# A transformer layer on one core: GpSimd adds the projection bias between its two normalisations, ScalarE copies the router logits ahead of the next hT

## What is computed

```python
q, k, v = jnp.moveaxis(qkv, 2, 0)
attn = jnp.einsum('bhnd,bhmd->bhnm', q, k) * SCALE
attn = attn * (1.0 - temperature[None] * eye)
attn = jax.nn.softmax(attn, axis=-1)
out = jnp.einsum('bhnm,bhmd->bhnd', attn, v)
out = out.transpose(0, 2, 1, 3).reshape(b, n, c)
return out @ w_proj + b_proj
...
h = _layernorm(h + _L0_attn_ref(h, ...), axis=-1)
...
scores = jnp.sqrt(jax.nn.softplus(flat @ gate_w))
_, indices = jax.lax.top_k(scores + gate_bias, K)
```

## Time and profile before

| | |
|---|---|
| runs | 801.5, 804.45, 809.3 us; median 804.45 |
| span of the profiled execution, first to last instruction | 762.7 us |
| PE (TensorE matmul) busy | 625.1 us, 82% |
| DVE (VectorE) busy | 480.6 us, 63% |
| ACT (ScalarE) busy | 321.7 us, 42% |
| POOL (GpSimd) busy | 189.1 us, 25% |
| mean granted TensorE clock | 0.896 |

### The profile page before, as it was taken

The page is one execution under the profiler, slowest core; times in us unless marked ns, Lnnn a source line. Parts: engine busy times, 40 slices in busy tenths (PEclk is TensorE's granted clock), DMA queues, the critical chain, the costliest instruction groups (busy, mean ns, idle before and its releaser), DMA issues.

```text
span 762.7 us, 15902 instructions
## 1 busy us (share of the span) xinstructions
PE 625.1 (82%) x4762; PEld 463.4 (61%) x4763; DVE 480.6 (63%) x1125; ACT 321.7 (42%) x564; POOL 189.1 (25%) x162
## 2 busy tenths in 40 slices
PE   4979788979797975488887999999999999999600
PEld 2665656756665665365655777777777777777500
DVE  0365756466757576557696566666666666677816
ACT  1433534444454545254533354444544445444200
POOL 1121524142424242423775000000000000006752
PEclk9989895989898987588999899999999999999855
DMA  6141422233333323242222011111111111112213
GB/s 250 52 161 38 140 90 89 76 119 90 119 90 119 90 72 105 79 131 60 82 83 71 23 42 43 36 36 36 41 43 36 36 36 40 44 37 71 79 52 97
DMA packets 51383, 57.85 MB, mean 76 GB/s; under 512 B 14544, under 2 KB 47728, under 8 KB 50080
## 3 DMA queue, kind: packets, MB, share of 16 engines
q1 hardware_dynamic: 47792, 50.22, 21.7%
q0 software_dynamic: 3568, 7.33, 3.3%
HBM read 41.78 MB, written 15.75 MB: 75 GB/s over the span
## 4 chain that ended last, share of the span: by engine, by line
PE 47%; issue 27%; POOL 14%; DVE 6%; ACT 2%; DMA 2%; POOLq 1%; SPq 0%; DVEq 0%; ACTq 0%
PE bank L632 20%; PE bank L651 9%; POOL dbuf L1434 5%; PE bank L642 5%; POOL stage L1450 4%; PE bank L500 4%; POOL arena L1376 3%; PE bank L485 2%; PE bank L540 2%; PE bank L558 2%; PE bank L620 1%; DMA con<-consts 1%; DVE arena L910 1%; POOL arena L1385 1%; DVE arena L948 1%
## 5 line engine op out<-in xcount | busy, mean ns | idle before, releaser
L632 PE MATMUL bank<-W,arena 128*128 (+1 forms) x1220 | 212.7, 331 | 0.0
L632 PEld LDWEIGHTS bank<-W,arena 128*128 128x128 f16 x1220 | 120.9, 99 | 74.7 <-issue 4.7
L651 PE MATMUL bank<-W,arena 128*128 (+1 forms) x1098 | 103.7, 250 | 8.9 <-DVE arena L1123 8.9
L1450 POOL DMA_INDIRECT stage<-ybuf,pos x36 | 36.1, 1002 | 287.6 <-DMA ybuf<-arena 277.0
L651 PEld LDWEIGHTS bank<-W,arena 128*128 128x128 f16 x1098 | 94.4, 100 | 17.9 <-DVE arena L1123 10.3
L1123 DVE SCALAR_TENSOR_TENSOR arena<-bank,sct,arena 128x384 f16<-128x384 f32 x86 | 49.1, 612 | 74.8 <-ACT arena L840 74.8
L485 PE MATMUL bank<-arena,par 128*96 128x288 f32 x192 | 69.0, 452 | 10.5 <-DMA con<-consts 10.1
L1137 DVE SCALAR_TENSOR_TENSOR arena<-arena 128x384 f32<-128x384 f32 x122 | 68.1, 558 | 4.2
L834 ACT ACTIVATE arena<-bank,sct 128x384 f32<-128x384 f32 x86 | 50.0, 581 | 43.1 <-PE bank L632 41.6
L642 PE MATMUL bank<-con,arena 128*128 128x128 f32 x366 | 54.5, 282 | 13.8 <-issue 8.2
L1132 DVE TENSOR_SCALAR arena<-bank,sct 128x384 f32<-128x384 f32 x86 | 58.2, 677 | 9.3 <-PE bank L632 9.1
(11 more groups left out here) (146 smaller groups left out, 883.4 us busy)
## 6 DMA issues: line engine op xcount, KB each, us to landing
stage<-w_all SPq DMA_DIRECT2D x9, 1344.0 KB, 6.0
arena<-xT SPq DMA_DIRECT2D x8, 864.0 KB, 4.9
stage<-w_all SPq DMA_DIRECT2D x9, 768.0 KB, 4.9
arena<-dbuf SPq DMA_DIRECT2D x43, 96.0 KB, 1.9
ybuf<-arena SPq DMA_DIRECT2D x43, 96.0 KB, 1.6
dbuf<-arena SPq DMA_DIRECT2D x6, 672.0 KB, 6.4
xbuf<-arena SPq DMA_DIRECT2D x8, 216.0 KB, 2.3
arena<-xbuf SPq DMA_DIRECT2D x18, 96.0 KB, 2.0
```

What stands on the lines that cost most here:

```text
L632: m = pe.matmul(bank[2 * k + n][:, 0:I // 2], xT16[:, b, lo, tail, :], W16[:, bass.ds(off + at + col, I // 2)], start=(z == 0), stop=(z == ...
L651: m = pe.matmul(bank[6][:, 0:C], hhT[:, lo, ic, :], W16[:, bass.ds(off + at + ic * C, C)], start=(ic == 0 and z == 0), stop=(ic == IC - 1 ...
L1450: PO.indirect_dma_start(fin[:, k % FS, c, :], None, ybuf[:, :], bass.IndirectOffsetOnAxis(ap=pos[:, c, k:k + 1], axis=0)).then_inc(s_f[k % ...
```

## The change

Two steps move; nothing is added or removed.

1. GpSimd's `h0b_out(g)` moves from the end of group g-1 (behind `weights_sum(g)`) into group g, between `normalise(g, 0)` and `normalise(g, 1)`. For group 0 it moves from the start of the program to the same place in group 0.
2. ScalarE's `logits_out(g-1)` moves ahead of `hT_out(g+1)`.

```diff
@@ ScalarE
                 weights_hi(g, (0,))
+                if not start:
+                    logits_out(g - 1)
                 if not last:
                     hT_out(g + 1)
-                if not start:
-                    logits_out(g - 1)
                 exps(g, 1)
@@ GpSimd
             def group(g, start=False, last=False):
                 normalise(g, 0)
+                h0b_out(g)
                 normalise(g, 1)
                 if not start:
                     scores_sqrt(g - 1)
...
                 if not last:
                     weights_sum(g + 1)
-                    h0b_out(g + 1)
-
-            h0b_out(0)
+
             weights_sum(0)
             group(0, start=True)
```

## The result

The changed kernel takes **823.85 us** (median of 4 runs, 816.66 to 828.54) against 806.88 us (4 runs, 801.5 to 809.7) of the kernel before: ratio **1.0203, interval 1.0136 to 1.0269**. The forecast was 812.0 with a range from 800.5 to 819. The profiled execution of the changed kernel took 819.69 us, its span is 817.9. Timed again later against the kernel before it took 779.88 us (773.08 to 790.13) against 767.53 (757.94 to 775.88), ratio 1.0177, interval 1.0097 to 1.0257. It is slower by about 2%, twice. Ratios and their intervals leave out runs more than 1.5% above the fastest of the same kernel; medians and ranges are of all runs.

What follows compares the result with a forecast made beforehand. It took the attention turn to be bound by GpSimd's chain, then VectorE, nearly tied with TensorE. Groups 1 to 6 net +9.3, group 0 +0.7, group 7 -2.5: +7.5 us on 804.45 gives 812.0 us, range 800.5 to 819.

Steps and rivals of the forecast that it cites:

- before's one long turn: Group 2 of the kernel before: clock stayed at 0.50, turn 44.00 us; its 6.0 us excess was subtracted from the sum.
- GpSimd's R stays: R is when GpSimd is free after the weights' sum, 7.08 us behind it; moving the bias was priced at nothing there.
- Transposes some 1.3 us behind R, second hole of 2.5 to 3: TensorE, groups 1 to 6: transposes start earlier, after the first normalisation, then wait 2.5 to 3 us before the projection.
- Projection at 4.05 in its first run, a fast turn of +1.4: TensorE, groups 1 to 6: first projection wholly at 1.2 GHz, 4.05 instead of 3.20 us; +1.4 us per group.
- too late for it: Clock returning 3.6 to 4.4 us after the first projection starts would not speed that projection, 4.05 us at 1.2 GHz.
- How often the clock stays down: Groups 1 to 6: one in four turns, 1.5 long episodes, each 4.6 us over a +1.4 turn.
- Group 0 at +0.7: Group 0: hT of group 1 newly waits for the bias, second exponentials come 0.5 to 1.0 us later; +0.7 us.
- Group 7 at -2.5: Last group: first normalisation no longer behind the bias, TensorE starts 2.4 to 4.2 us earlier; -2.5 us.
- Long episodes in most groups: Rival: clock fails to return in four of six groups' second runs; +19 us, 823.5 us, chance 0.1.
- The clock survives: Rival: TensorE's clock does not fall over two short holes, no turn is cold; -4.3 us, 800 us, chance 0.12.

Runs made afterwards that it cites:

- bias first: Kernel before, with GpSimd's bias ahead of the weights' sum instead of behind it: 762.21 against 767.53 us, ratio 0.9973.
- logits only: Kernel before, with only ScalarE's copy of the logits moved ahead of hT and GpSimd's order kept: 799.23 against 803.03 us, ratio 0.998.
- last group only: Kernel before, with the bias between the two normalisations in the last group alone: one run, 752.6 us against a median of 767.53.
- only GpSimd's half: Changed kernel with hT ahead of the logits again, so only the bias is moved: 820.72 against 803.03 us, no ratio.
- one hole instead of two: Changed kernel with one more wait: TensorE waits for hT ahead of the transposes, so they join the projection: 810.97 against 803.03 us, ratio 1.012.
- two holes filled: Changed kernel with useless identity transposes, 10 behind the router and 19 between transposes and projection: 809.92 against 803.03 us, ratio 1.0116.
- three holes filled: Changed kernel with identity transposes in TensorE's two holes and also ahead of the second half's transposes: 770.37 against 764.21 us, no ratio with an interval.
- sum on TensorE: Kernel before, with two matmuls with a matrix of ones replacing GpSimd's reduction for groups 0 to 7: 745.36 against 764.21 us, ratio 0.9769.
- filler in the kernel before: Kernel before with the logits ahead of hT and 34 identity transposes between router and transposes: 765.82 against 764.21 us, ratio 0.9989.
- router moved: Kernel before with the weights' sum on TensorE, logits ahead of hT, router matmuls ahead of the last score matmul: 749.03 against 767.53 us, ratio 0.981.
- the three kernels without its reduction: Weights' sum on TensorE: in the kernel before (0.9769), in the changed kernel (0.9708), in the kernel before with early logits and earlier router matmuls (0.981).

## Why the prediction was wrong, step by step

The sum of my terms was +7.5 us. To the root of group 7 the profiles give +18.4.

| term | forecast | profile | again |
|---|---|---|---|
| group 0 | +0.7 | +4.3 | +5.5 |
| fast turns of groups 1 to 6, 6 x (mean of the fast - 37.55) | +8.4 | +7.4 | +7.6 |
| long turns' excess over the fast | 1.5 x 4.6 = +6.9 | 3 x 4.96 = +14.9 | 2 x 4.82 = +9.6 |
| before's one long turn | -6.0 | -6.45 | -6.45 |
| group 7 | -2.5 | -1.75 | -2.6 |
| sum | +7.5 | +18.4 | +13.6 |

(37.55 is the mean of before's five fast turns. The fast turns of the changed kernel average 38.79 in the first profile, 38.81 in the second; 43.75 and 43.64 are its long ones. Group 0 again: 65.84 - 60.39; group 7 again: 35.78 - 38.37.)

- **GpSimd's R stays**: right. 14.49 against 14.47 us behind the root; the experiment with the bias first shows 6.70 us behind the sum with no bias there.
- **Transposes some 1.3 us behind R, second hole of 2.5 to 3**: the first right in four of six turns (1.28 to 1.29 us), 1.78 in group 3 (163.41 - 161.63, behind a normalisation of 1.64) and 1.68 in group 5. The second hole is 1.76 to 3.00. That the transposes are slow in every turn was wrong: in three of six they ran at 0.93 to 1.03.
- **Projection at 4.05 in its first run, a fast turn of +1.4**: right in size (+1.24), and four of the seven fast turns of both profiles (38.93 to 39.86) went as told, with the clock back in the second run. Wrong in "too late for it": in the other three (38.03 to 38.43) the clock comes back at the end of the first projection (group 4: L500 4.06, then L558 1.39), which I had ruled out.
- **How often the clock stays down**: this is the step that failed. "One in four, for six groups" gave 1.5 long turns; the profiles have 3 and 2 of six. I counted eight cold runs of before with two failures, but those runs were transposes and projection unbroken, behind one hole. The fraction belonged to a pattern that the change abolishes, and I carried it over without a row of the new one. Four profiles in the old order (before, logits only, bias first, last group only) have 2 long turns in 24; the two of the changed kernel 5 in 12. The cut of the run isn't the whole reason: joined again, with the bias still moved, the clock missed the first projection in five of six turns.
- **Group 0 at +0.7**: failed too. I priced the later exponentials and put the clock at nothing, though the earlier trace rows show a cold run there and hT was a new wait. The clock stayed down in it: +4.3 and +5.5. The root is at 64.68 to 67.73 us in the four profiles with the bias moved, the sum on GpSimd and no filler, and at 60.38 and 59.39 with filler. Of the 10.9 us that the first profile has beyond the forecast the long turns are 8.0, group 0 is 3.6, the fast turns are -1.0 and the rest is 0.3.
- **Group 7 at -2.5**: right sign, -1.75 and -2.6; the normalisation took 2.73 us beside L1065 in the first profile, so it is the late end of my bounds that came. The last-group-only kernel has -1.6.
- **The rivals.** "Long episodes in most groups" (four of six, 823.5, chance 0.1) is nearest to what came: three of six and group 0, then two of six and group 0. That its 823.5 meets the 823.85 is in part luck: its sum of +19 stands against +18.4 and +13.6. Its chance was too low, and the forecast's own range ended at three episodes. "The clock survives" falls: the first projection is slow in the long turn and in the fast one (4.18, 4.06). The Trainium skill (TensorE: Matmul & The Clock Gate, "Why this matters for your kernels") advises against idle gaps above about 3 us; here the two gaps of 2.48 and 1.76 us were both under that and the run behind them was at 0.50 for 19.5 us, so gaps below that figure are not safe here, and the measurement decides.

**What is shown and what is not.** One profile of each kernel; roots and turns in us:

| profile | root of group 0 | mean turn, groups 1 to 6 | last root |
|---|---|---|---|
| before | 60.39 | 38.62 | 330.51 |
| only ScalarE's half | 60.76 | 37.50 | 324.21 |
| only GpSimd's half | 67.73 | 40.50 | 346.16 |
| changed | 64.68 | 41.27 | 348.93 |
| changed, again | 65.84 | 40.42 | 344.14 |
| one hole instead of two | 65.96 | 41.03 | 349.20 |
| two holes filled | 60.38 | 39.87 | 336.31 |
| three holes filled | 59.39 | 39.55 | 332.08 |

Shown in the profiles: the loss is in GpSimd's half; ScalarE's half alone is at 0.998. Shown as far as single profiles can: the clock is the larger part. From ScalarE's half alone to the changed kernel the last root moves by 24.7 and 19.9 us, and three fillers, which remove no dependence, take back 16.9 and 12.1 of them. The 7.9 us that stay are the new order's dependences, the filler and the clock's fall at another place, and no run separates these. The run times alone don't show it: the kernel with three fillers has no interval.

Not shown: that cutting TensorE's run in two is the cause. Joining the runs gave nothing back in its profile. Not settled: what decides whether the clock comes back within an unbroken run. A rival that the rows leave open is the length of the wait ahead: in the six profiles with transposes and projection in one run (before, both halves alone, bias first, last group only, one hole) the first projection took its full 4.05 us in 1 of 24 turns behind holes of 3.46 to 5.12 us, and in 8 of 12 behind holes of 5.34 to 7.28 us; eleven of these twelve are of kernels with the bias moved. No run changes the length and nothing else. The same kernel has a long turn in group 3 in one profile and a fast one there in the other; slow first transposes went ahead of all five long turns, but of two others as well. Open too: where the stalls of the expert stage come from.

## What to carry to other kernels

Where TensorE's clock falls at a wait, a shift that moves or splits the wait can cost more than its dependences: price its turns with the clock down, too. A frequency counted in the old order (how often the clock returned) is no frequency of the new one; if the pattern of holes changes, put the likeliest case at the bad end and the range with it. Test the reason apart from the number: filler brought most of the time back, joining the run did not. And look behind the wait for its cause: no order of GpSimd's work gained anything that a measurement could tell, while the three kernels without its reduction of 0.41 us in each group gained 1.9% to 2.9%.

## What the runs showed of the hardware that I had not expected

- **The clock can fall behind a hole under 2 us.** 0.54 us (sum on TensorE, behind the router's 12 small matmuls, 1.19 us), 0.73 and 1.69 (three holes filled), 1.28 (filler in the kernel before), 1.67 (GpSimd's half), 2.25 (two filled), 2.27 (router moved). In the kernel before, 1.68 us ahead of the output projection cost nothing in any turn. So the length of the last hole alone doesn't tell.
- **The clock can stay at 0.50 under unbroken work** for 19.5 us, with L500, L558 and L511 at 4.05, 2.49 and 5.49 us.
- **GpSimd's reduction costs on both sides**: 5.8 to 6.1 us of "issue" ahead of it and 6.7 to 7.6 us behind it before the next ordinary instruction, some 13 us of surroundings for 0.41 us of work, in each turn that was read. The trace has `MODIFY_POOL_CONFIG` records at both places: in group 3 of the changed kernel at 148.2 us, 5.8 ahead of the sum, and again at 154.4, 7.2 ahead of the normalisation (in the kernel before at 217.9 and 224.2, ahead of the sum and of the bias). The Trainium skill (GPSIMD Engine Reference, "Instruction dispatch") gives about 6 us from such a record to a freshly loaded kernel's first call. The trace agrees in size ahead of the sum; here it comes with each sum, and the way back to the ordinary instructions takes the 6.7 to 7.6 us.
- **A faster TensorE meets a new wait**: each filled hole moved the clock's fall to another wait in the turn; none of the 18 turns of groups 1 to 6 in the three filled kernels is without one. The filler is not free either: 34 transposes take 3.91 us at full clock, and the transposes behind them still waited 1.23 us.
